# Second GAT attention by pairs of heads, with h2 stationary and the product turned back

## The reference, cut to what matters

```
def gat_conv(x, src, dst, W, att_src, att_dst, bias, heads, out_ch):
    h = (x @ W).reshape(N, heads, out_ch)
    a_src = jnp.einsum('nhc,hc->nh', h, att_src)
    a_dst = jnp.einsum('nhc,hc->nh', h, att_dst)
    e = jax.nn.leaky_relu(a_src[src] + a_dst[dst], NEG_SLOPE)
    m = jax.ops.segment_max(e, dst, num_segments=N)
    ...
    ex = jnp.exp(e - m[dst])
    s = jax.ops.segment_sum(ex, dst, num_segments=N)
    alpha = ex / (s[dst] + 1e-16)
    msg = h[src] * alpha[:, :, None]
    out = jax.ops.segment_sum(msg, dst, num_segments=N)
    return out.reshape(N, heads * out_ch) + bias
```

## Time and profile before

| what | us |
|---|---|
| median of three runs | 1790.54 (1788.01 to 1790.7) |
| the profiled execution's own time | 1782.27 |
| its span | 1780.4 |
| second GAT attention, first `ramp` to last `save_out` | 522.65 to 804.66, 282.01 |
| PE busy over the span | 1635.2 (92%) |
| DVE busy over the span | 1307.7 (73%) |
| ACT busy over the span | 1164.9 (65%) |

### The profile page before, as it was taken

One profiled execution on the slowest core, in us unless ns is written; L12 is line 12 of the kernel. 1 busy time (PEld: TensorE's weight loads), 2 busy tenths in 40 slices (PEclk: granted clock), 3 DMA queues, 4 the chain that ended last, 5 costly groups with the idle time before them and its releaser, 6 DMA issues. The chain is left out here.

```text
span 1780.4 us, 34835 instructions
## 1 busy us (share of the span) xinstructions
PE 1635.2 (92%) x14082; PEld 1511.8 (85%) x14082; DVE 1307.7 (73%) x2329; ACT 1164.9 (65%) x2102; POOL 37.3 (2%) x53
## 2 busy tenths in 40 slices
PE   6898999999979999998979999998797999999971
PEld 3786999999859999998968888888796888888871
DVE  6995999997568999877247778756722777777577
ACT  3454788898648888776447788772433778887323
POOL 0000000000000000000000000002000000000020
PEclk9999899999989999899989999999898999999995
DMA  5113223200025221104964234003077133200204
GB/s 178 53 57 99 71 74 103 83 30 1 1 60 168 88 88 59 59 1 119 259 152 119 59 79 96 2 11 120 1 181 199 63 76 71 66 2 1 60 0 122
DMA packets 73355, 139.33 MB, mean 78 GB/s; under 512 B 16269, under 2 KB 44773, under 8 KB 71912
## 3 DMA queue, kind: packets, MB, share of 16 engines
q1 hardware_dynamic: 73192, 137.06, 27.4%
HBM read 96.22 MB, written 29.45 MB: 71 GB/s over the span
## 5 line engine op out<-in xcount | busy, mean ns | idle before, releaser
L1017 PE MATMUL banks<-h,probs_t_gat 125*125 125x128 f32 (+1 forms) x3200 | 376.2, 274 | 0.0
L1017 PEld LDWEIGHTS banks<-h,probs_t_gat 125*125 125x125 f32 x3200 | 367.2, 191 | 0.0
L2022 DVE CUSTOM_DVE_ANT_0 probs_att<-banks,logs_or_y 125x1250 f32<-125x1250 f32 x160 | 233.6, 1460 | 147.8 <-PE banks L1926 146.6
L1982 ACT COPY probs_t_att<-banks 125x375 f32<-125x375 f32 (+1 forms) x480 | 205.4, 533 | 76.3 <-PE banks L1936 76.2
L1974 ACT ACTIVATE probs_att<-probs_att,neg_max_att 125x1250 f32<-125x1250 f32 x160 | 218.4, 1365 | 49.6 <-DVE neg_max_att L2022 49.6
L1003 PE MATMUL banks<-ident,probs_gat 125*125 125x125 f32 x1600 | 214.7, 283 | 20.6 <-ACT probs_gat L1091 20.6
L1235 DVE CUSTOM_DVE_ANT_0 probs_gat<-probs_gat,log_counts 125x1250 f32<-125x1250 f32 x160 | 232.7, 1455 | 0.1
L1091 ACT ACTIVATE probs_gat<-probs_gat,neg_max_gat 125x1250 f32<-125x1250 f32 x160 | 212.8, 1330 | 20.5 <-DVE neg_max_gat L1235 20.0
L1003 PEld LDWEIGHTS banks<-ident,probs_gat 125*125 125x125 f32 x1600 | 195.3, 196 | 24.4 <-ACT probs_gat L1091 24.3
L1936 PE MATMUL banks<-ident,probs_att 125*125 125x125 f32 x1600 | 191.4, 275 | 0.0
L1100 ACT COPY probs_t_gat<-banks 125x1250 f32<-125x1250 f32 x160 | 190.0, 1188 | 2.1 <-PE banks L1003 2.1
(11 more groups left out here) (231 smaller groups left out, 2548.2 us busy)
## 6 DMA issues: line engine op xcount, KB each, us to landing
a_pair<-a_src_rows SPq DMA_DIRECT2D x46, 625.0 KB, 4.8
q_first<-q_rows SPq DMA_DIRECT2D x12, 1000.0 KB, 10.8
logs_or_y<-log_rows SPq DMA_DIRECT2D x20, 546.9 KB
q_rows<-q_out_qkv SPq DMA_DIRECT2D x40, 250.0 KB, 4.5
q_att<-q_rows SPq DMA_DIRECT2D x8, 1000.0 KB, 10.6
w_rows<-in_L_gnn_W_dram SPq DMA_DIRECT2D x12, 512.0 KB, 14.5
log_counts<-counts_fr SPq DMA_DIRECT2D x50, 122.1 KB
k_halves<-k_low_qkv SPq DMA_DIRECT2D x20, 250.0 KB, 4.2
```

Of the source, the lines that this page charges most:

```text
L1017: total = pe.matmul(out_bank(u), probs_t[:, u % KEPT, i], rows, start=i == 0, stop=i == T - 1)
L1982: act.copy(probs_t[:, u % TURNED, lo:hi].rearrange("p c n -> p (c n)"), turned(u, j)).then_inc(piece_saved, 1)
L2022: dve.tensor_tensor_reduce(probs[:, u % SLOTS], scores, logs[:, t % KEPT], -1.0, -FLOOR, ALU.add, ALU.min, neg_max[:, column(u)]).then_inc ...
```

## The change

Units are now numbered so that two heads alternate: for an even u, u and u+1 are heads 2k and 2k+1 of one tile, a pair. `weigh_pair` makes h2 the stationary operand (64 columns) and streams the turned probabilities (125 columns), once for each head of the pair, the even head into PSUM partitions 0 to 63 and the odd head into 64 to 127 of one bank, `cols_bank`. The product is now turned (columns by nodes), so it is copied to SBUF by DVE (`copy_out`, 128 x 125), turned back by one transpose on PE (`turn_back`) and then scaled by ACT, a head at a time (`save_pair`). `cols_bank` is a single bank: each `weigh_pair` waits for the `copy_out` of the pair before.

`a_pair` gets a third slot and `probs_t` a fourth for this layer; a head's rows are loaded when the head three before has ramped its last unit. The small columns (`neg_max`, `sums`, `inverse`) become a ring of 16. The first layer keeps its order. Some early steps begin 3 units later (`TOP_AT` = LATER + 11 in place of 8, and so on).

```diff
+    COLUMNS = 16
+    KEPT2, SLOTS = 4, 3
+    WIDTH = 2 * (w2.shape[1] // H)
...
             if u < LATER:
-                return 1, (u - PER) // A, (u - PER) % A
-            return 1, (u - LATER) // (T - A), A + (u - LATER) % (T - A)
+                pair = (u - PER) // 2
+                return 1, pair // A * 2 + u % 2, pair % A
+            pair = (u - LATER) // 2
+            return 1, pair // (T - A) * 2 + u % 2, A + pair % (T - A)
...
+        cols_bank = k.psum[0:WIDTH, 6 * BANK:6 * BANK + P]
+        back_bank = k.psum[0:P, 7 * BANK:7 * BANK + WIDTH]
...
             load_pair(1, 1)
+            load_pair(1, 2)
...
-            for part in range(2, 2 * H):
-                sp.wait_ge(ramp_done, first_unit(part - 1))
-                load_pair(1, part % H)
+            for part in range(SLOTS, 2 * H):
+                sp.wait_ge(ramp_done, last_unit(part - SLOTS) + 1)
+                load_pair(1, part)
...
+            def weigh_pair(u):
+                pair, head = pairs_before(u), place(u)[1]
+                pe.wait_ge(probs_saved, u + 2)
+                if pair >= 1:
+                    pe.wait_ge(out_copied, pair)
+                for i in range(T):
+                    for odd in range(2):
+                        total = pe.matmul(cols_bank[odd * CH[1]:(odd + 1) * CH[1]],
+                                          h2[:, i, (head + odd) * CH[1]:(head + odd + 1) * CH[1]],
+                                          probs_t_slot(u + odd)[:, i], start=i == 0, stop=i == T - 1)
+                total.then_inc(summed, 1)
+
+            def turn_back(u):
+                pair = pairs_before(u)
+                pe.wait_ge(out_copied, pair + 1)
+                if pair >= 1:
+                    pe.wait_ge(final_done, u)
+                pe.transpose(back_bank, out_cols[:, pair % 2], k.ident[0:WIDTH, 0:WIDTH]).then_inc(turned_back, 1)
...
-            for n in range(PER, UNITS + 2):
-                if n < UNITS:
-                    turn(n)
-                if n >= PER + 2:
-                    weigh(n - 2)
+            for u in range(PER, UNITS + 6, 2):
+                if u < UNITS:
+                    turn(u)
+                if u >= PER + 6:
+                    turn_back(u - 6)
+                if u < UNITS:
+                    turn(u + 1)
+                if PER + 2 <= u < UNITS + 2:
+                    weigh_pair(u - 2)
...
+            def save_pair(u):
+                _, head, t = place(u)
+                act.wait_ge(turned_back, pairs_before(u) + 1)
+                act.wait_ge(inverted, u + 2)
+                for odd in range(2):
+                    act.activation(gat.g[:, t, (head + odd) * CH[1]:(head + odd + 1) * CH[1]],
+                                   back_bank[:, odd * CH[1]:(odd + 1) * CH[1]], ACT.Copy, scale=inverse[:, column(u + odd)]
+                                   ).then_inc(final_done, 1)
...
-                if n >= PER + 3:
-                    save_out(n - 3)
+                if n >= PER + 8 and n % 2 == 0:
+                    save_pair(n - 8)
...
+            def copy_out(u):
+                pair = pairs_before(u)
+                dve.wait_ge(summed, PER + pair + 1)
+                if pair >= 2:
+                    dve.wait_ge(turned_back, pair - 1)
+                dve.tensor_copy(out_cols[:, pair % 2], cols_bank).then_inc(out_copied, 1)
...
                     if layer == 1:
+                        if n >= PER + 6 and n % 2 == 0:
+                            copy_out(n - 6)
```

More of the change, by code:

```diff
@@ L897, in stage_gat @@
                                                   "next_high_done", "next_low_done"))
-        a_loaded = [k.sem(f"a_loaded{i}_gat") for i in range(2)]
+        third_pair = gat.at("third_pair_gat", [128, 2, N], F32, turned_w + 8 * D + 448)
+        fourth_probs_t = gat.at("fourth_probs_t_gat", [P, T, P], F32, turned_w + 8 * D + 448 + gat.padded(8 * N))
+        out_cols = gat.at("out_cols_gat", [WIDTH, 2, P], F32, spare + gat.padded(8 * T * H) + gat.padded(4 * T * H))
+        out_copied, turned_back = k.sem("out_copied_gat"), k.sem("turned_back_gat")
+        a_loaded = [k.sem(f"a_loaded{i}_gat") for i in range(SLOTS)]
         w_loaded = [k.sem(f"w_loaded{c}_gat") for c in range(K // 2)]
@@ L918, in place, with last_unit, pairs_before, column @@
             if u < LATER:
-                return 1, (u - PER) // A, (u - PER) % A
-            return 1, (u - LATER) // (T - A), A + (u - LATER) % (T - A)
-        def first_unit(part):
-            return PER + part * A if part <= H else LATER + (part - H) * (T - A)
+                pair = (u - PER) // 2
+                return 1, pair // A * 2 + u % 2, pair % A
+            pair = (u - LATER) // 2
+            return 1, pair // (T - A) * 2 + u % 2, A + pair % (T - A)
+        def last_unit(part):
+            tiles, base = (A, PER) if part < H else (T - A, LATER)
+            return base + 2 * (part % H // 2 * tiles + tiles - 1) + part % 2
+        def pairs_before(u):
+            return (u - PER) // 2
+        def column(u):
+            return slice(u % COLUMNS, u % COLUMNS + 1)
+        def rows_slot(layer, part):
+            if layer == 0:
+                return gat.pair[:, part % 2]
+            return gat.pair[:, part % SLOTS] if part % SLOTS < 2 else third_pair
+        def probs_t_slot(u):
+            if u < PER:
+                return probs_t[:, u % KEPT]
+            return probs_t[:, u % KEPT2] if u % KEPT2 < KEPT else fourth_probs_t
+        def loads_before(layer, part):
+            if layer == 0:
+                return part // 2
+            earlier = 3 if part % SLOTS < 2 else 0
+            return earlier + sum(1 for p in range(1, part + 1) if p % SLOTS == part % SLOTS)
         def live(layer, n):
@@ L1007, in weigh @@
             def weigh(u):
-                layer, head, _ = place(u)
+                _, head, _ = place(u)
                 pe.wait_ge(probs_saved, u + 1)
@@ L1088, in exponential @@
             def exponential(u):
-                t = place(u)[2]
                 act.wait_ge(masked, u + 1)
-                act.activation(probs[:, u % PROBS], probs[:, u % PROBS], ACT.Exp, scale=-1.0, bias=neg_max[:, t:t + 1],
-                               accum_out=sums[:, t:t + 1]).then_inc(exp_done, 1)
+                act.activation(probs[:, u % PROBS], probs[:, u % PROBS], ACT.Exp, scale=-1.0, bias=neg_max[:, column(u)],
+                               accum_out=sums[:, column(u)]).then_inc(exp_done, 1)
             def save_turned(u):
@@ L1097, in save_turned @@
                     act.wait_ge(a_stored, 32)
-                if u >= KEPT:
+                if PER > u >= KEPT:
                     act.wait_ge(summed, u - KEPT + 1)
-                act.copy(probs_t[:, u % KEPT].rearrange("p (b c) n -> p b (c n)", c=2), turned(u)).then_inc(probs_saved, 1)
+                if u >= PER + KEPT2:
+                    act.wait_ge(summed, PER + pairs_before(u - KEPT2) + 1)
+                act.copy(probs_t_slot(u).rearrange("p (b c) n -> p b (c n)", c=2), turned(u)).then_inc(probs_saved, 1)
             def save_out(u):
-                layer, head, t = place(u)
+                _, head, t = place(u)
                 act.wait_ge(summed, u + 1)
                 act.wait_ge(inverted, u + 1)
-                cols = slice(head * CH[layer], (head + 1) * CH[layer])
-                result = (gat.rows, gat.g)[layer][:, t, cols]
-                act.activation(result, out_bank(u), ACT.Copy, scale=inverse[:, t:t + 1]).then_inc(final_done, 1)
+                result = gat.rows[:, t, head * CH[0]:(head + 1) * CH[0]]
+                act.activation(result, out_bank(u), ACT.Copy, scale=inverse[:, column(u)]).then_inc(final_done, 1)
+            def save_pair(u):
+                _, head, t = place(u)
+                act.wait_ge(turned_back, pairs_before(u) + 1)
[4 more added lines that the diff above has]
+                                   ).then_inc(final_done, 1)
             def cut_w(c):
@@ L1196, in _ @@
             save_spread(2)
-            for n in range(PER, UNITS + 3):
+            for n in range(PER, UNITS + 7):
                 if n < UNITS:
@@ L1218, in ramp @@
                     part = head + H * (t > 0)
[L1219 to L1222, removed]
+                    before = loads_before(layer, part)
+                    if before and (layer, part) != (1, 0):
+                        dve.wait_ge(a_loaded[part % (2, SLOTS)[layer]], 32 * before)
+                    elif layer == 0:
                         dve.wait_ge(gat.spread[head], 32)
@@ L1228, in ramp @@
                     dve.wait_ge(probs_turned, u - PROBS + 1)
-                dve.scalar_tensor_tensor(probs[:, u % PROBS], gat.pair[0:P, head % 2, 0], (gat.gap1, gap2)[layer][:, t, head:head + 1],
-                                         gat.pair[0:P, head % 2, 1], ALU.add, ALU.max).then_inc(ramp_done, 1)
+                rows = rows_slot(layer, head + H * (u >= LATER))
```

(4 more changed lines are left out.)

26 lines of the change are left out of this document (11 added, 15 removed).

## The result

The change makes the kernel slower: 1808.13 us median of four runs (1803.94 to 1809.36), against 1789.28 (1786.38 to 1790.7) for the kernel before on the same chip. The ratio is 1.0119, 95% interval 1.0094 to 1.0144. The prediction was 1818 with a range of 1797 to 1848. The profiled execution's own time is 1809.36, its span 1807.6; before they were 1782.27 and 1780.4.

A forecast was written before the change was run, and what follows sets the result against it. PE, busiest before, gives way to a loop through DVE's copy, 6.96 us a pair against 6.54. The stage ends 12.3 us later without the clock, plus 15 for its falls: 27.4 on 1790.54, so 1818, range 1797 to 1848.

The forecast's parts named there:

- loop copy, weighing, turning, ramp, mask, copy: Second GAT attention: PE's weighing waits for DVE's copy, DVE's ramp for PE's turning; 6.96 us a pair against 6.54.
- weighing to the next load: PE's weighing of a pair in 40 shorter loads, 2.30 us, read from the transformer's attention of the same form.
- the copy: DVE's copy of 128 x 125 out of PSUM, taken as 0.29 us between bounds 0.2 and 0.48.
- a round: One pass of the loop for a pair in the second GAT attention: 6.96 us (6.87 to 7.15), 35 of them.
- rounds with a fall of the clock: PE's clock falls after 2.0 us of idle time in nine loops, 1.7 us each, 15 us; bounds 0 and 35.
- other steps that no idle time hides: DVE's maxima, additions and statistics overrun by 4.1 us, plus 0.3 for ACT's table loads: 4.4 us.
- last ramp's round to the stage's end: Three more weighings, the last turnings, copies, turnings back and scalings, one behind the other: 17.7 us.
- the halves don't run side by side: Rival, chance 0.02: weighing's 40 loads take 4.36 us, the loop 9.0, 35 x 2.06 more: 1875.
- The start: Second GAT attention: the second ramp waits for head 1's rows by DMA until 528.8, 3.2 us lost; first copy ends 550.9.
- the offset: The median of the kernel before stands 8.3 us above its profiled execution; added to the changed kernel's 1809.6.
- The clock holds: Rival, chance 0.15: PE's clock doesn't fall in the idle times of 2.0 us; kernel at 1803.
- Stays low: Rival, chance 0.02: PE's clock stays low through the stage, doubling the loop's PE part, 128 us more: 1930.

The follow-up runs named there:

- e1: The changed kernel with DVE's copy of the turned product made one pair earlier, nothing else moved; 1771.09 us, ratio 0.9932 to the kernel before.
- e4: The changed kernel with all ten products of a pair's even head first, then the odd head's, not by turns; 1913.26 us, ratio 1.0724 to the kernel before.
- e5: The changed kernel with DVE making each copy of the turned product twice, the extra result unused; 1821.42 us, ratio 1.0210 to the kernel before.
- e3: The changed kernel with the second unit of each pair turned twice, ten extra transposes on PE; 1801.98 us, ratio 1.0099 to the kernel before.
- e6: The kernel with the copy one pair earlier (e1), but ACT makes the copies in place of DVE; 1761.58 us, ratio 0.9868 to the kernel before.

## Why the prediction was right, and what was mis-sized

The mechanism was right: the loop copy, weighing, turning, ramp, mask, copy; once a pair; with PE's idle time in one piece, released by the copy. The trace shows it and e1 confirms it by taking the loop apart. The stage's size came out nearer than its terms were, in part by luck, and the absolute time was 10 us too high. Term by term:

| step of the prediction | said | measured |
|---|---|---|
| copy done to weighing's first load | 0.06 | 612.52 - 612.40 = 0.12 |
| weighing to the next load | 2.30 | 2.33 |
| turning | 1.35 | 1.36 |
| turning's end to ramp | 0.03 | 0.03 |
| ramp to copy | 2.93 | 619.20 - 616.24 = 2.96 |
| the copy | 0.29 | 0.27 |
| a round | 6.96 | 7.06 to 7.07 |
| wait at the second ramp, against 525.60 - 522.65 in the earlier trace rows | ramp at 528.8 | 530.48 |
| first copy ends | 550.9 | 552.61 |
| rounds with a fall of the clock, and each | 9, 1.7 | 7, 1.6 |
| other steps that no idle time hides | 4.4 | 3.2 |
| last ramp's round to the stage's end | 17.7 | 17.7 |
| PE's idle time a round | 2.0 | 2.21 to 2.27 |
| stage's end later by | 27.4 | 26.05 |

- **The weighing.** 2.33 at the pace of the transformer's attention; e4 shows that this pace rests on the alternation of the two heads, which the row itself doesn't show. The rival in which the halves don't run side by side is wrong for after; e4, which takes the alternation away, lengthens a round by 1.74, against the 2.06 that the rival took.
- **The copy.** Bounds 0.2 and 0.48, taken 0.29 by ACT's row of the same shape; measured 0.27. Only 0.19 of it delays DVE's next instruction (e5), but the weighing waits for its end, so 0.27 is right in the loop.
- **The start.** The load of head 1 took longer than I had worked out from the earlier trace rows: 1.7 us. The later loads are hidden, as said, but for 0.07 in the rounds in which a pair of heads begins (7.13 against 7.06).
- **The clock.** The prediction took nine falls at 1.7, 15 us. Measured seven: six cost 1.6, and the seventh, in a round which other work lengthens anyway (8.17 in e3, 8.75 here), 0.6. Together 10.2. The 3.4 us of one fall stands in no row, has windows of 3.2 and 10.1; in after's trace PEclk is 0.50 from 620.88 to 624.29, 3.41. The low edge was well read, 1.27 of idle time passed there and 2.2 fell in some rounds, but the rows didn't give their number and the nine was a choice between 0 and 35; that it came near seven is luck.
- **The sum.** Without falls the stage's end should come 12.3 later; it came 26.05 - 10.2 = 15.9 later. The 3.5 are 1.7 of the start and 1.8 of the rounds: 35 x 0.10 = 3.5, less 1.2 that the other steps took less than said and 0.4 of rounding. So two errors of 4 and 5 us, the pace with the start and the falls, had opposite signs, and the stage's 27.4 against 26.05 is in part luck.
- **The step that was mis-sized is the offset.** I took 8.3 us from the profiled execution of before to its median and added them to the changed kernel. The profile of after ran 1.2 above its own median (1809.36 and 1808.13); the profile's own time plus the 27.4 would have given 1809.7. The offset isn't a property of the program: in the two later measurements before ran from 1778.36 to 1790.75 with mean clocks of 0.957 to 0.948, the longer times at the lower clocks, and after's four runs from 1803.94 to 1809.36. The median of before over the 25 runs of all three measurements is 1786.5, so the three runs behind 1790.54 lay high. The other side of it is that the difference of the medians is 18.8 and not 27.4. Whether the longer executions of before spend their 8 us in this stage, where the change would take their place, or elsewhere, stays open: none of them has a trace.
- **The rivals.** "The clock holds" (1803) has nearly the time of e3 (1801.98, one fall), but the 1803 carries the offset of 8.3. "Stays low": after's stage has a mean PEclk of 0.92, and the granted clock is 1.00 in rounds of e3 in which 30 of the 71 matmuls are transposes:

```profile
608.55:615.61 7.06, 5.95 (x71) 1.00 0.01 3
610.85:614.51 3.66, 3.65 (x33) 1.00 0.00 0
```

Both are windows of e3, PE alone; the second holds the 30 transposes, one turning back and the last two matmuls of the weighing. The Trainium skill, TensorE: Matmul & The Clock Gate, Part 4, says the full clock doesn't engage for transposes. Here it held through 3.65 us of them, and ten more of them a round, in PE's idle time, left no fall in the rounds with 1.11 of it. So in this kernel the clock stayed up through them, and the measurement decides against the rule. Whether transposes alone would bring it up from 1.2 GHz no run shows.

## What to carry to other kernels

Before a change that makes the busiest engine quicker by handing its result to another engine, follow the new wait round: what is queued behind it, and does the copy's own engine wait for that? Here a loop of 7.06 us took the place of 6.54 us of plain work, and moving one copy two units earlier made a loss of 19 us a gain of 13. Once DVE was the bound, each 0.19 us of its time in a pair came back in the kernel's time, so what another engine has room for belongs there. And a gap between one profiled execution and the median needn't be there in the next kernel: here the profile lay 7.0 below the median before and 1.2 above it after, so a difference of two traces (27) and one of two medians (18.8) can be 8 us apart, and it takes more than one trace to say which the change makes.

## What was not expected of the hardware

- More work on TensorE didn't make the kernel slower (e3): with 400 transposes more the stage is 8 us shorter in the trace. Behind 1.1 to 1.2 us of idle time the clock fell in none of e3's rounds, its one fall standing behind 2.62; behind 2.2 it fell in five of after's.
- The length of the idle time alone doesn't say how often the clock falls. With 2.20 to 2.28 it fell in five of the 31 rounds of after that have it and in 30 of the 34 of e4, whose round is longer; with 2.40 to 2.47 in eight of the 30 of e5. These rows of e4 (PE's timeline) show the same idle time ahead of a weighing, first in a round where the clock held and then in one where it fell:

```profile
570.66 2.01 PE L1061 MATMUL banks<-probs_t_gat,h 125*64 125x125 f32 x17 [2.21 <-DVE out_cols_gat L1318]
579.46 5.74 PE L1061 MATMUL banks<-probs_t_gat,h 125*64 125x125 f32 x40 [2.21 <-DVE out_cols_gat L1318]
```

What decides between the two stays open; no run here separates it.

- The order of the same 40 loads and matmuls on the two column halves is worth 1.74 us: 2.33 by turns against 4.07 one half behind the other.
- Shorter idle times did no harm: e1 and e6 leave PE idle for up to 0.99 and 0.76 in their plain rounds, and in none of those did the clock fall. e1's three falls stand behind 1.40, 1.58 and 2.25, and others of 1.40 to 1.92 passed.
